# A decoder's first stage: prefix ratio kept where its inputs are and read one element to the left, second normalisation finished on ScalarE

## What is computed

```python
gate_x = sigmoid(block_diag_linear(x, w_in, b_in))
gate_a = sigmoid(block_diag_linear(x, w_a, b_a))
a = minimum(exp(-gate_a * (softplus(a_param) + MIN_DECAY)), 1 - EPS)
normed_x = x * gate_x * sqrt(maximum(1 - a * a, EPS))
p_prefix = maximum(concatenate([ones, cumprod(a)[:, :-1]]), SCAN_EPS)
h = p_prefix * cumsum((normed_x + SCAN_EPS) / p_prefix)
x = layernorm(x + h)                                     # first normalisation
q, k, v = xpos(x @ Wq), xpos(ctx @ Wk), ctx @ Wv
x = layernorm(x + ((q @ k.T) * decay_mask) @ v)          # second normalisation
```

## Time and profile before

| | |
|---|---|
| median of 3 runs | 1648.25 us (1647.36 to 1651.45) |
| the profiled execution | 1658.71 us, of which the span of its records is 1656.9 us |
| busy in the span | PE 1521.7, VectorE 1144.9, ScalarE 802.8, GpSimd 583.2 us |
| first stage, last scan (L824) of the loop starts | at 225.00 us |

### The profile page before, as it was taken

One profiled execution on the slowest core, in us unless ns is written; L12 is line 12 of the kernel. 1 busy time (PEld: TensorE's weight loads), 2 busy tenths in 40 slices (PEclk: granted clock), 3 DMA queues, 4 the chain that ended last, 5 costly groups with the idle time before them and its releaser, 6 DMA issues.

```text
span 1656.9 us, 34388 instructions
## 1 busy us (share of the span) xinstructions
PE 1521.7 (92%) x12742; PEld 1356.0 (82%) x12742; DVE 1144.9 (69%) x2350; ACT 802.8 (48%) x1527; POOL 583.2 (35%) x684
## 2 busy tenths in 40 slices
PE   3888898899999999788888699999989999999997
PEld 2777777799999999776777488888879999989997
DVE  3899987655655565137888458878866868676674
ACT  5777732244554455236666445445434444443442
POOL 3666650222211220047775212121114444443443
PEclk9999999899999999999999799999999999999999
DMA  6222253212323330152233411212135463544443
GB/s 189 64 79 80 73 183 121 77 55 74 100 92 101 101 102 26 51 197 77 85 94 96 144 61 53 78 53 71 35 73 109 88 130 83 116 101 96 101 94 68
DMA packets 118159, 152.11 MB, mean 92 GB/s; under 512 B 10090, under 2 KB 102852, under 8 KB 117508
## 3 DMA queue, kind: packets, MB, share of 16 engines
q1 hardware_dynamic: 110068, 127.48, 28.1%
q0 software_dynamic: 6560, 19.02, 4.0%
q10 hardware_dynamic: 1392, 3.70, 0.6%
HBM read 111.37 MB, written 38.80 MB: 91 GB/s over the span
## 4 chain that ended last, share of the span: by engine, by line
PE 39%; ACT 5%; DVE 5%; issue 5%; DMA 3%; SPq 1%; POOL 1%; DVEq 0%; ACTq 0%; POOLq 0%
PE psum L531 14%; PE psum L1811 4%; PE psum L1447 3%; PE psum L1795 3%; PE psum L498 3%; PE psum L506 3%; PE psum L1789 2%; PE psum L1772 2%; DMA arena_x<-wT_d 2%; ACT arena_y L1543 1%; DVE psum L2381 1%; ACT arena_y L1558 1%; PE psum L490 1%; PE psum L1492 1%; PE psum L1479 1%
## 5 line engine op out<-in xcount | busy, mean ns | idle before, releaser
L2152 POOL TENSOR_TENSOR d_g_parts<-arena_w,d_g_parts 128x512 fp32r<-128x512 f32 x128 | 167.1, 1305 | 253.5 <-ACT d_g_parts L2284 249.8
L531 PE MATMUL psum<-d_v_high,d_g_parts 128*128 128x256 f32 x1024 | 205.6, 284 | 3.3 <-DVE arena_x L1944 2.8
L531 PE MATMUL psum<-d_x_parts,d_v_high 128*128 128x256 f32 x1024 | 195.1, 288 | 6.7 <-issue 5.0
L531 PE MATMUL psum<-m_w_high,m_h_parts 128*128 128x256 f32 x1024 | 188.0, 284 | 0.0
L1213 ACT ACTIVATE arena_x<-psum,b_e 128x512 f32<-128x512 f32 x128 | 88.2, 689 | 190.2 <-PE psum L531 92.2
L531 PEld LDWEIGHTS psum<-d_v_high,d_g_parts 128*128 128x128 f32 x1024 | 168.5, 192 | 4.8 <-issue 3.0
L531 PEld LDWEIGHTS psum<-d_x_parts,d_v_high 128*128 128x128 f32 x1024 | 160.4, 193 | 13.7 <-issue 7.9
L1141 POOL DMA_INDIRECT arena_x<-x_d,slot_row x64 | 67.7, 1058 | 293.3 <-PE psum L1187 229.0
L531 PE MATMUL psum<-m_xF_parts,m_w_high 128*128 128x512 f32 x512 | 160.2, 394 | 2.1 <-DVE m_xF_parts L526 2.1
L531 PEld LDWEIGHTS psum<-m_w_high,m_h_parts 128*128 128x128 f32 x1024 | 160.7, 192 | 0.0
L531 PE MATMUL psum<-d_x_parts,d_vd_low 128*128 128x256 f32 x512 | 145.6, 284 | 0.0
(11 more groups left out here) (281 smaller groups left out, 3700.1 us busy)
## 6 DMA issues: line engine op xcount, KB each, us to landing
arena_x<-wT_d SPq DMA_DIRECT2D x128, 256.0 KB, 6.2
arena_y<-in_L_ffn_w SPq DMA_DIRECT2D x16, 1024.0 KB, 7.9
x_d<-arena_x SPq DMA_DIRECT2D x32, 256.0 KB, 2.2
y_d<-arena_x SPq DMA_DIRECT2D x16, 512.0 KB, 8.9
arena_x<-kv_d SPq DMA_DIRECT2D x16, 512.0 KB, 3.4
kv_d<-arena_x SPq DMA_DIRECT2D x9, 512.0 KB, 2.9
arena_x<-in_x SPq DMA_DIRECT2D x16, 256.0 KB, 2.9
arena_x<-in_ctx SPq DMA_DIRECT2D x16, 256.0 KB, 3.0
```

The costliest lines, as they stand in the source:

```text
L531: ins = nc.tensor.matmul(dst, left[a_], right[b_], start=start and k == 0, stop=stop and k == 2, skip_group_check=True)
L2152: nc.gpsimd.tensor_tensor(K["gP"][:, s % 4, 1], K["g"][:, s % 2], K["gP"][:, s % 4, 0].bitcast(F32), ALU.subtract).then_inc(d_gl, 1)
```

## The change

In the first stage, the ratio gets a tile of 8 + 512 elements. VectorE writes it at its inputs' positions (512 contiguous elements for 508 in four pieces), a memset then zeroes the last element of each segment, and the scan reads the tile one element to the left. The second normalisation is no longer applied on VectorE: the three helpers that exist are moved up and used for it, with a wait on `a_x2` of the unit before added in front of L828, and with `ln_result` put at the end of ScalarE's step.

```diff
-        for n in ("u", "r", "t1", "t2"):
+        for n in ("u", "t1", "t2"):
             A[n] = arena_x.take([P, NC_, T])
+        PAD = 8
+        A["ratio"] = arena_x.take([P, PAD + NC_ * T])
...
-        A_st2 = sb("A_st2", [P, UB, 10])
+        A_st2 = sb("A_st2", [P, UB, 12])
...
-                    done(act, a_r, u1.back(2))
+                    done(act, a_r, u1.back(2), 2)
...
                     nc.scalar.activation(A["xF"][:, u0.p], chunks(bank(2)), ACT.Copy).then_inc(a_xF, 1)
+                if u5:
+                    done(act, aT_x2, u5.back(2))
+                    landed(act, a_st, u5.back(2))
+                    ln_result(act, u5, A["r2"], A["x2"][:, u5.p], A_st2, ln2)
...
+                    ratio, ratio_before = A["ratio"][:, PAD:], A["ratio"][:, PAD - 1:PAD - 1 + NC_ * T]
...
-                    nc.vector.tensor_tensor(quads(A["r"])[:, :, 1:S], quads(A["a"][:, p])[:, :, 0:S - 1],
-                                            quads(A["u"])[:, :, 0:S - 1], ALU.max).then_inc(a_r, 1)
+                    nc.vector.tensor_tensor(ratio, flat["a"], flat["u"], ALU.max).then_inc(a_r, 1)
+                    dve.wait_ge(a_r, u2.n * 2 + 1)
+                    nc.vector.memset(ratio.rearrange("p (n s) -> p n s", s=S)[:, :, S - 1:S], 0.0).then_inc(a_r, 1)
...
-                    done(dve, a_r, u2)
-                    nc.vector.tensor_tensor_scan(flat["h"], flat["r"], flat["h"], 0.0, ALU.mult,
+                    done(dve, a_r, u2, 2)
+                    nc.vector.tensor_tensor_scan(flat["h"], ratio_before, flat["h"], 0.0, ALU.mult,
                                                  ALU.add).then_inc(a_h, 1)
                 if u5:
                     done(dve, a_ret, u5)
+                    done(dve, a_x2, u5.back(1))
                     nc.vector.tensor_tensor(A["r2"][:, :, :], seqs(bank(6)), A["x1"][:, u5.p],
                                             ALU.add).then_inc(a_r2, 1)
...
-                    ln_stats(dve, u5, A["r2"], A_st2, ln2)
+                    ln_bn(dve, u5, A["r2"], A_st2, ln2)
+                    ln_moments(dve, u5, A_st2, ln2)
+                    ln_shift(dve, u5, A_st2, ln2)
...
-                if u5:
-                    done(dve, aT_x2, u5.back(2))
-                    landed(dve, a_st, u5.back(2))
-                    ln_apply(dve, u5, A["r2"], A["x2"][:, u5.p], A_st2, ln2)
...
-                    rstd(pool, u5, A_st2, ln2)
+                    root_and_shift(pool, u5, A_st2, ln2)
```

More of the change, by code:

```diff
@@ L484, in rstd, with ln_shift, root_and_shift, ln_result @@
             nc.gpsimd.tensor_tensor(stats[:, :, 8:9], stats[:, :, 9:10], minus_half[:, :, :], ALU.pow).then_inc(s_rs, 1)
+        def ln_shift(dve, u, stats, sems):
+            done(dve, sems[0], u, 2)
+            done(dve, sems[2], u.back(1), 2)
+            nc.vector.tensor_scalar(stats[:, :, 9:10], stats[:, :, 7:8], LN_EPS, None, ALU.add)
+            nc.vector.tensor_scalar(stats[:, :, 10:11], stats[:, :, 6:7], -1.0, None, ALU.mult).then_inc(sems[1], 1)
+        def root_and_shift(pool, u, stats, sems):
+            done(pool, sems[1], u)
+            done(pool, sems[3], u.back(1))
+            nc.gpsimd.tensor_tensor(stats[:, :, 8:9], stats[:, :, 9:10], minus_half[:, :, :], ALU.pow).then_inc(sems[2], 1)
+            pool.wait_ge(sems[2], u.n * 2 + 1)
+            nc.gpsimd.tensor_tensor(stats[:, :, 11:12], stats[:, :, 10:11], stats[:, :, 8:9],
+                                    ALU.mult).then_inc(sems[2], 1)
+        def ln_result(act, u, src, dst, stats, sems):
+            done(act, sems[2], u, 2)
+            for b in range(UB):
+                ins = nc.scalar.activation(dst[:, b, :], src[:, b, :], ACT.Identity, scale=stats[:, b, 8:9],
+                                           bias=stats[:, b, 11:12])
+            ins.then_inc(sems[3], 1)
         def to_feature(dst, src):
@@ L713, in step @@
             def step(t):
-                u0, u1, u2, u3, u4, u6 = (t.at(k, UNITS) for k in (0, 1, 2, 3, 4, 6))
+                u0, u1, u2, u3, u4, u5, u6 = (t.at(k, UNITS) for k in range(7))
                 if u2:
@@ L797, in step @@
                     flat = {n: A[n][:, p].rearrange("p c t -> p (c t)") for n in ("inv", "h")}
-                    flat |= {n: A[n].rearrange("p c t -> p (c t)") for n in ("u", "r")}
+                    flat["u"] = A["u"].rearrange("p c t -> p (c t)")
+                    flat["a"] = A["a"][:, p].rearrange("p c t -> p (c t)")
+                    ratio, ratio_before = A["ratio"][:, PAD:], A["ratio"][:, PAD - 1:PAD - 1 + NC_ * T]
                     done(dve, a_thx, u2)
@@ L848, in step @@
                                             ALU.max).then_inc(a_cap, 1)
-                if u5:
-                    done(dve, aT_x2, u5.back(2))
-                    landed(dve, a_st, u5.back(2))
-                    ln_apply(dve, u5, A["r2"], A["x2"][:, u5.p], A_st2, ln2)
             for p in range(2):
                 nc.vector.memset(quads(A["inv"][:, p])[:, :, 0:1], BIG).then_inc(a_init, 1)
-            nc.vector.memset(quads(A["r"])[:, :, 0:1], 0.0).then_inc(a_init, 1)
+            nc.vector.memset(A["ratio"][:, 0:PAD], 0.0).then_inc(a_init, 1)
             dve.wait_ge(a_init, 3)
@@ L1381, in c_sync @@
             pipelined(sp, UNITS, C_LAG, step, unroll=4)
[L1383 to L1405, removed]
         def c_gpsimd(pool):
```

## The result

| | before | after |
|---|---|---|
| median of 10 runs each | 1648.11 us (1642.96 to 1651.45) | 1655.01 us (1651.41 to 1659.40) |
| ratio of the runs | | 1.0043, 95% interval 1.0031 to 1.0056 |
| the profiled execution's span | 1656.9 us | 1649.6 us |
| from the scan of step 5 to that of step 17 | 163.69 us | 170.05 us |
| from there to the router's first reduction | 38.25 us | 36.90 us |

The change makes the kernel slower by about 7 us. (Three executions behind these and all later figures, one each of E2, of E11 and of the kernel before beside E5 to E8, took 105 us or more longer than their neighbours and are left out.) The two profiled executions stand the other way round, by 7 us. The first stage is longer in the trace of after too; what is shorter is the rest: from the router's first reduction to the end it is 1382.3 us for 1393.7.

The account below looks back on a forecast made before the run. VectorE was taken to bound the 13.66 us step, then the four-engine loop at 13.81. Steps came to +0.7, step 17 without its fall made -0.4, and one to two falls +1.5 to +3.0: 1648.25 + 1.9 = 1650 us, range 1644 to 1660.

Parts of the forecast that it names:

- the clock rival: First stage, TensorE: its clock falls in most steps after 1.5 us waits; eight falls give 1660 us, four 1654; chance 0.17.
- The bound passes from VectorE to the four-engine loop: First stage: VectorE's 13.66 us set the old step; a loop through four engines, 13.14 us before, sets the new at 13.81.
- The ratio waits for GpSimd, not for its layout: VectorE, first stage: the ratio takes 1.62 us behind GpSimd's product and 0.69 when GpSimd stands still, same pieces.
- The ratio goes first in the new step: VectorE: ratio starts near 1.9 us after ScalarE's square, done by 2.6, before GpSimd's product; GpSimd's second operation falls to 1.04.
- The step, 13.81 predicted: First stage's new step: 5.08 us from square to scan, 7.74 from scan to square, 0.99 for two Identity activations on ScalarE.
- the start of the scan: VectorE: scan starts 5.08 us after ScalarE's square, because GpSimd ends at 5.04.
- The fall of step 17 goes away: TensorE, step 17: its wait shortens by about 1 us; without the clock fall about 1.15 us return, -0.4 in all.
- The number of falls: TensorE's clock in 11 steps: bounds none to one in each; one to two taken, about 1.5 us each, +1.5 to +3.0.
- Sum: Whole kernel: +1.1 to +2.6 us, middle +1.9, giving 1650; the profiled execution would read 1660.6.

Follow-up runs that it names:

- E2: Kernel before with only the second normalisation moved to ScalarE as two Identity activations, ratio in its old four pieces: 1655.24 us, ratio 1.0048.
- E11: Kernel before with reordered VectorE and GpSimd work, Identity activations before the copy of v, old ratio, epsilon addition behind the key's rotation products: 1655.99 us, ratio 1.0046.
- E5: The changed kernel run once more, unaltered, on the second chip beside the kernel before: 1655.61 us, ratio 1.0037.
- E8: Kernel before, reordered only: VectorE does g, prefix scan, ratio before first normalisation's statistics; GpSimd does its root after both h operations: 1643.55 us, ratio 0.9966.
- E9: Changed kernel with the two Identity activations of the second normalisation done twice at the end of ScalarE's step: 1676.82 us, ratio 1.0179.
- E3: Changed kernel with the two Identity activations moved on ScalarE from the step's end to before the copy of v: 1650.48 us, ratio 1.0019.
- E1: Kernel before with only the ratio's part (512 contiguous elements, memset, shifted read), second normalisation kept on VectorE: 1651.81 us, ratio 1.0025.
- E7: Changed kernel with Identity activations before the copy of v, VectorE's ratio before first normalisation's statistics, GpSimd's root after its h operations: 1640.90 us, ratio 0.9952.
- E4: Changed kernel with 8 filler matmuls on the identity in TensorE's wait before the transposes of x1, all steps from 6 on: 1655.34 us, ratio 1.0042.
- E10: Kernel before with Identity activations before the copy of v, reordered VectorE and GpSimd work, ratio in its old four pieces, no memset: 1648.25 us, ratio 1.0002.
- E6: Changed kernel with 8 filler matmuls on the identity in TensorE's wait before the transposes of x1, steps 6 to 15 only: 1657.65 us, ratio 1.0046.

## Why the prediction was right or wrong

The time, 1655, lies in the range of 1644 to 1660 and 2 us above the forecast's own 1646 to 1653. The direction that I gave 0.30 came out, and "same" (0.58) didn't. That the wide range held is owed to the clock rival, not to the middle of the sum. The profiled execution was to read 1660.6 us and reads 1651.4: the kernel before's own, 10 us above its median, was the odd one.

- **The bound passes from VectorE to the four-engine loop: right for the new step, half right for the old one.** It was read from 0.52 us to spare in the loop and 0.99 for the pair. E9 doubles the pair and the step grows by 0.92, as it must on the loop. But the 0.52 were to spare only beside the ratio's wait for GpSimd. With that wait in it the loop took the old step's whole 13.66 us, and E3 shows it: 1.1 us less on VectorE make no shorter step than E1's. Not VectorE's length but the ratio's place was what could be gained from, as E8 found.
- **The ratio waits for GpSimd, not for its layout: right**, by E1 and E2 from both sides. The Trainium skill (SBUF — State Buffer, Who interferes with whom) gives the same rule; E3 and E7 agree with it, 1.62 against 0.69 us by who starts first.
- **The ratio goes first in the new step: right.** It starts 1.86 us after the square (1.9 predicted), and GpSimd's second operation is at 1.04.
- **The step, 13.81 predicted, 13.93 measured.** The term that was small is the start of the scan: 5.16 to 5.24 us after the square, not 5.08. The other two are right (8.74 us from scan to square, 8.73 predicted). In E2, without memset and shifted read, it is 5.06 to 5.15: there the scan starts 0.03 us after GpSimd's end, in the changed kernel 0.12. I had put the shifted read at nothing or up to 0.1, but it isn't shown that the 0.1 is the read's: in the first unit and in steps 7, 16 and 17 the changed kernel's scan starts after 0.03 us too. What delays it in between is open. In eleven steps, clean of falls, the growth above the forecast is 0.8 us.
- **The fall of step 17 goes away: right**, 36.90 us to the router's reduction for 38.25, in after and in E5. E2 has a longer one there (40.23 us).
- **The number of falls was the term with the widest bounds, and set low.** I took one to two of 1.5 us. The two profiled executions of the changed kernel have three and one in these steps, of 1.54 to 1.70 us. The rival of eight falls was not this kernel, but E9 showed that it is only one microsecond of waiting away.
- **Sum.** The stage grew by 5.3 us (after) and 3.6 us (E5) in the traces, for 1.9 predicted. In after the falls are 4.9 us for 1.5 to 3.0, and steps and start together 1.0 more than forecast. In E5 one fall lies in these steps and another, of 1.7 us, before them. The timed runs say 7. The 1.6 to 4 us between are not found: they lie behind the stage, where one and the same code differs by up to 14 us between traces, and that I had counted as unchanged. E4 warns how much that can be: no falls, a stage only 2.4 us longer than before in its trace, and still 6.9 us in the time.

## What to carry to other kernels

Before work is moved off the busiest engine, measure the loop behind it, with the waits of one engine for another in it: here it had 0.5 us to spare at best, and the pair that was moved onto it cost 1.0. Look at the order of who starts first before looking at shapes, when an operation takes twice its own shortest record: a few moved lines gave 4.5 us (E8), which the new layout couldn't, though E10 shows the same steps without a gain in time. And watch what the new order does to the matmul engine's waits; two short ones that become one of 1.5 us can cost more than their sum.

## What the runs showed of the hardware

- TensorE's clock fell from 2.4 to 1.2 GHz behind waits of 1.4 to 1.8 us in 1 to 3 of 11 steps (after, E5, E2), behind waits of 2.0 to 2.65 us in 8 of 11 (E9), and also once behind 1.09 us (E8) and once behind 1.23 us (E11). Each time it stayed low for 3.4 us. With two waits of 0.7 to 1.1 us in a step it never fell in the middle of the stage (before, E1, E3). The neighbours of the wait were short transposes and 8-column matmuls.
- An operation on two elements per partition took 1.08 us instead of 0.17 when GpSimd had started a 1.27 us operation 0.2 us before it (E7). It ends with GpSimd's (137.50 and 137.48 us): the price is what is left of GpSimd's operation, whatever the waiting one's own length.
- Eight 128x128 float32 matmuls on the identity show as 16 records and fill 1.84 us (E6), so 0.23 us for one, where four transposes of that shape take 0.44 together (0.11 each).
